# Two float32r parts and paired 64-row matmuls in the attention of a decoder block

## The reference, cut to what matters

```
B, L, D = 4, 1024, 256;  16 heads of 16;  context of 154 tokens;  FFN of 1024
nx = ln(x);  q, k, v = heads(nx @ W_qkv)
x  = x + softmax(q k^T / 4, causal) v @ W_self_out
q  = heads(ln(x) @ W_q);  k, v = heads(context @ W_kv)
x  = x + softmax(q k^T / 4) v @ W_cross_out
x  = x + relu(ln(x) @ W1 + b1) @ W2 + b2
```

## Time and profile before

| | |
|---|---|
| runs | 1325.73 us median of 3 (1321.71 to 1331.97) |
| span of the profiled execution | 1319.6 us (its own time isn't listed beside it) |
| PE busy | 1073.5 us (81%), 7120 matmuls |
| DVE, ACT, POOL busy | 829.3, 644.7, 436.7 us |
| DMA | 115.33 MB, 27% of 16 engines |
| longest entries of the chain | issue 26%, DMA max_rows<-nm 9%, PE L756 8%, PE L737 7% |

### The profile page before, as it was taken

How to read it: one execution, slowest core, us unless ns; L and a number is a source line. 1 busy time by engine, 2 the same in 40 slices (tenths; PEclk the granted TensorE clock), 3 DMA queues, 4 the chain that set the end, 5 groups by cost and what they waited for, 6 DMA issues and landing times.

```text
span 1319.6 us, 23773 instructions
## 1 busy us (share of the span) xinstructions
PE 1073.5 (81%) x7120; PEld 610.3 (46%) x7120; DVE 829.3 (63%) x1489; ACT 644.7 (49%) x1354; POOL 436.7 (33%) x677
## 2 busy tenths in 40 slices
PE   4837768899899989999999574776666889989997
PEld 3625543344344434444337331322222348888886
DVE  6739556688688868888429552543534576666552
ACT  4614335576576756777764242443434572322321
POOL 8624241233233323322334220111111135555443
PEclk9969887899899989999999786877867898999999
DMA  5635333212212221215128431221121311111110
GB/s 160 217 111 147 113 130 105 76 50 86 70 67 78 71 78 62 90 61 178 42 88 264 160 98 51 67 67 60 55 67 60 110 50 48 48 49 62 32 33 32
DMA packets 84521, 115.33 MB, mean 87 GB/s; under 512 B 13632, under 2 KB 70752, under 8 KB 79712
## 3 DMA queue, kind: packets, MB, share of 16 engines
q1 hardware_dynamic: 84416, 114.02, 27.0%
HBM read 71.49 MB, written 42.51 MB: 86 GB/s over the span
## 4 chain that ended last, share of the span: by engine, by line
PE 36%; issue 26%; DMA 17%; POOL 9%; DVE 7%; ACT 3%; SPq 3%; POOLq 0%; DVEq 0%; ACTq 0%
DMA max_rows<-nm 9%; PE bank L756 8%; PE bank L737 7%; PE bank L630 6%; DMA k_st<-k_parts 4%; PE bank L612 3%; PE bank L614 3%; PE bank L613 3%; POOL hT_lo L1516 3%; ACT probs L996 2%; DVE nx_mem L1091 2%; PE bank L633 2%; DMA q_st<-qx_parts 1%; DMA qx_parts<-probs 1%; DVE stats L1080 1%
## 5 line engine op out<-in xcount | busy, mean ns | idle before, releaser
L1105 DVE TENSOR_REDUCE mx<-bank 128x1 f32<-128x512 f32 (+5 forms) x784 | 468.1, 640 | 259.6 <-PE bank L630 133.8
L996 ACT ACTIVATE probs<-bank 128x512 f32<-128x512 f32 (+4 forms) x1024 | 462.6, 518 | 337.6 <-PE bank L737 316.3
L737 PE MATMUL bank<-q_st,k_st 128*128 128x512 bf16 (+4 forms) x1024 | 342.9, 366 | 117.8 <-DMA q_st<-max_rows 100.2
L630 PE MATMUL bank<-k_st,q_st 125*128 125x154 bf16 (+4 forms) x1280 | 311.7, 307 | 74.0 <-DMA k_st<-k_parts 44.7
L737 PEld LDWEIGHTS bank<-q_st,k_st 128*128 128x128 bf16 (+1 forms) x1024 | 102.1, 107 | 338.7 <-ACT probs L996 171.2
L756 PE MATMUL bank<-probs,nx_mem 128*32 128x512 f32 (+4 forms) x2048 | 250.0, 562 | 3.8 <-DVE oT L1181 2.8
L630 PEld LDWEIGHTS bank<-k_st,q_st 125*128 125x128 bf16 x1280 | 129.2, 106 | 149.9 <-DMA k_st<-k_parts 45.6
L1444 POOL TENSOR_SCALAR_AFFINE_SELECT probs<-probs 128x256 f32<-128x256 f32 x256 | 101.2, 407 | 243.1 <-ACT probs L996 240.5
L1516 POOL TENSOR_TENSOR hT_lo<-hT,hT_hi 128x512 fp32r<-128x512 f32 x64 | 93.1, 1474 | 93.4 <-DVE hT_hi L1315 93.4
L1453 POOL TENSOR_TENSOR oN<-oT,rs 128x256 f32<-128x256 f32 x64 | 40.5, 633 | 218.0 <-DVE rs L1186 216.0
L633 PE MATMUL bank<-causal_bf,ident_bf 128*128 128x128 bf16 x512 | 103.7, 227 | 0.0
(11 more groups left out here) (124 smaller groups left out, 1421.0 us busy)
## 6 DMA issues: line engine op xcount, KB each, us to landing
xt<-in_x_dram SPq DMA_DIRECT2D x16, 512.0 KB, 4.9
q_parts<-probs SPq DMA_DIRECT2D x16, 384.0 KB, 3.2
k_parts<-probs SPq DMA_DIRECT2D x16, 384.0 KB, 2.8
q_st<-q_parts SPq DMA_DIRECT2D x16, 384.0 KB
k_st<-k_parts SPq DMA_DIRECT2D x16, 384.0 KB
qx_parts<-probs SPq DMA_DIRECT2D x16, 384.0 KB, 3.4
q_st<-qx_parts SPq DMA_DIRECT2D x16, 384.0 KB
v_aug<-vst_mem SPq DMA_DIRECT2D x8, 544.0 KB, 4.4
```

The costliest lines, as they stand in the source:

```text
L630: last = pe.matmul(bank[:, m, keys * j:keys * j + keys], q_st[w][0:MROWS, i, P * qb:P * qb + P], keys_of(a, w)[0:MROWS, i, k0:k0 + keys], ...
L737: pe.matmul(bank[0:a.kp, m, 0:n], keys_of(a, w)[:, i, a.kp * kb:a.kp * kb + a.kp], q_st[w][:, i, lo:lo + n], start=True, stop=True).then_i ...
L996: act.activation(probs[0:a.kp, use % NPT, 0:n], bank[0:a.kp, a.s_banks[use % a.SB], 0:n], ACT.Exp, scale=SCALE).then_inc(a.exp_done, 1)
L1105: dve.tensor_reduce(mx[:, par, part, blocks.start:blocks[-1] + 1:blocks.step], bank[:, m, 0:len(blocks) * keys].rearrange("p (q k) -> p q ...
```

## The change

q and k are held as two float32r parts; three products of parts (high-high, high-low, low-high) make 48 rows for a head instead of 96. So two heads lie above each other in a stack: head `j` of a pair in partitions 64j to 64j+47, with two rows (48, 49) for two parts of the negated maximum. Weight columns are put in another order for that (`ordered`, `heads`: each ordering is two instructions of half the width). ACT's `middle` and POOL's `lowest` go; DVE's `low` writes the second part itself. A row of a stack is 2 x 1024 x 4 bytes, again 8 KB (2 x 154 x 4 bytes for context keys); a store is 128 rows x 2 parts x 512 tokens x 4 bytes, 512 KB where it was 384 KB. The maxima tiles of a pair of heads go to two banks and one DVE instruction reduces both; S has 20 such units a stack and two units in the ring, X 6 and one unit; the early tiles have one. The masks are made by four bf16 matmuls of 64 rows for a pair. X's accumulator has two banks. DVE negates and splits the maxima in two steps; SP moves them by four DMAs from SBUF to SBUF with no wait between.

```diff
-    NPART = 3
-    Q_PARTS, K_PARTS = (0, 0, 0, 1, 1, 2), (0, 1, 2, 0, 1, 0)
...
+    NPART = 2
+    HALF = P // 2
+    KROWS = 3 * DK
+    KALL = KROWS + NPART
+    RUNS = {"q": ((0, 0, 2, True), (2, 1, 1, False)), "k": ((0, 0, 2, False), (2, 0, 1, False))}
...
-            stacks = [(sb_room(f"q_st{w}", [P, 4, L], BF16), sb_room(f"k_st{w}", [P, 4, L], BF16)) for w in range(4)]
+            stacks = [(sb_room(f"q_st{w}", [P, 2, L], F32R), sb_room(f"k_st{w}", [P, 2, L], F32R)) for w in range(4)]
...
-                            m = min(HF // keys, 4) if keys != 384 else 1
-                            self.tiles += [(range(8 * i + qb, 8 * (i + m), 8), k0, keys, k0 // HF) for i in range(0, 4, m)]
+                            m = min(HF // keys, 2)
+                            self.tiles += [(range(8 * i + qb, 8 * (i + m), 8), k0, keys, k0 // HF) for i in range(0, 2, m)]
...
-        SA = Attention("S", ..., [0, 1, 2], [3], [4, 5, 6, 7])
-        XA = Attention("X", ..., [0, 1, 4, 5], [6], [2, 3, 7])
+        SA = Attention("S", ..., [0, 1, 2], [3], [(4, 5), (6, 7)])
+        XA = Attention("X", ..., [0, 1, 4, 5], [6, 7], [(2, 3)])
-        EARLY_BANKS, EARLY_SLOTS, EARLY_FROM = 3, 12, 20
+        EARLY_UNITS, EARLY_SLOTS, EARLY_FROM = 1, 12, 20
-        EARLY_BANKS_X, EARLY_SLOTS_X, EARLY_FROM_X = 2, 5, 6
+        EARLY_UNITS_X, EARLY_SLOTS_X, EARLY_FROM_X = 1, 5, 6
...
 load_stacks:
-                    for r, first, count in RUNS[side] if side in sides else ():
-                        rows = one(src, u).rearrange("u s (g d i) t -> (u s) g d (i t)", g=2, d=DK)[:, w % 2]
-                        rows = rows[first:first + count] if side == "k" else rows[first:first + 1].to_broadcast([count, DK, 4 * n])
+                    for j in range(2):
+                        for r, first, count, repeated in RUNS[side] if side in sides else ():
+                            rows = one(src, u).rearrange("u s (g j d a) t -> (u s) g j d (a t)", g=2, j=2, d=DK)[:, w % 2, j]
+                            rows = rows[first:first + 1].to_broadcast([count, DK, 2 * n]) if repeated else rows[first:first + count]
+                            p0 = HALF * j + DK * r
...
 rows:
-                sp.wait_ge(a.nm_ready, v + 1)
-                sp.dma_start(max_rows[par].rearrange("s r t -> r s t"), nm[:, par]).then_inc(a.rows_out[par], 16)
-                sp.wait_ge(a.rows_out[par], 16 * (v0 // 2 + 2 * b + 1))
-                sp.dma_start(q_st[v0 % 4][MROWS:P, :, :],
-                             max_rows[par].rearrange("s (i q) t -> s i (q t)", i=4)).then_inc(a.rows_in[par], 16)
+                sp.wait_ge(a.m_free, a.turn_use(v0) + 4 * b * (a.MT + 1) + 1)
+                for j in range(2):
+                    for c in range(NPART):
+                        row = HALF * j + KROWS + c
+                        sp.dma_start(q_st[v0 % 4][row:row + 1, :, :].rearrange("s a (q t) -> s (a q) t", t=P).bitcast(F32),
+                                     nm[16 * j:16 * j + 16, par, c, :].bitcast(F32)).then_inc(a.rows_in[par], 16)
...
 max_tile on PE:
+                for y, (i, qb) in enumerate(divmod(x, 8) for x in blocks):
+                    for j in range(2):
+                        h0 = HALF * j
+                        last = pe.matmul(banks[:, j, keys * y:keys * y + keys], q_st[w][h0:h0 + KROWS, i, P * qb:P * qb + P],
+                                         keys_of(a, w)[h0:h0 + KROWS, i, k0:k0 + keys], start=True, stop=not masked)
                     if masked:
+                        for e0, width in ((HALF, P), (0, HALF)):
+                            for j in range(2):
+                                h0 = HALF * j
+                                last = pe.matmul(banks[:, j, end - width:end], eye[h0:h0 + HALF, e0:e0 + P],
+                                                 below[h0:h0 + HALF, 0:width], start=False, stop=width == HALF)
...
 scores:
-                    pe.matmul(bank[0:a.kp, m, 0:n], keys_of(a, w)[:, i, a.kp * kb:a.kp * kb + a.kp],
-                              q_st[w][:, i, lo:lo + n], start=True, stop=True).then_inc(a.st_ready, 1)
+                    rows = slice(HALF * (i % 2), HALF * (i % 2) + KALL)
+                    pe.matmul(bank[0:a.kp, m, 0:n], keys_of(a, w)[rows, i // 2, a.kp * kb:a.kp * kb + a.kp],
+                              q_st[w][rows, i // 2, lo:lo + n], start=True, stop=True).then_inc(a.st_ready, 1)
...
 slot on PE:
-                    for i in range(4):
-                        if v0 < 4 * B:
-                            scores(v0, b, s, i)
-                        for n in some[(len(some) * i + 3) // 4:(len(some) * (i + 1) + 3) // 4]:
+                    cut = len(some) - len(some) // 2
+                    for pair in range(2):
+                        if v0 < 4 * B:
+                            for i in range(2 * pair, 2 * pair + 2):
+                                scores(v0, b, s, i)
+                        for n in some[cut:] if pair else some[:cut]:
                             max_tile(a, v0 + 2, b, n, a.MB)
-                        if i == 1 and 0 <= q - LAG < 4 * B * a.NS:
+                        if pair == 0 and 0 <= q - LAG < 4 * B * a.NS:
                             weigh((q - LAG) // a.NS, b, (q - LAG) % a.NS)
...
 DVE:
-            def split(ph, use, dst, src, hi):
+            def low(ph, use, part, src):
                 dve.wait_ge(ph.hi_ready, use + 1)
-                dve.tensor_tensor(dst, src, hi, ALU.subtract).then_inc(ph.rest_ready, 1)
+                dve.tensor_tensor(part[:, 1, :], src, part[:, 0, :].bitcast(F32), ALU.subtract).then_inc(ph.lo_ready, 1)
...
-                dve.tensor_scalar(nmf[:, :], bank[0:32, m, 0:P], -1.0, None, ALU.mult).then_inc(a.m_free, 1)
+                dve.tensor_scalar(nm[:, par, 0, :], bank[0:32, m, 0:P], -1.0, None, ALU.mult).then_inc(a.nm_hi, 1)
+                dve.wait_ge(a.nm_hi, v + 1)
+                dve.scalar_tensor_tensor(nm[:, par, 1, :], bank[0:32, m, 0:P], -1.0, nm[:, par, 0, :].bitcast(F32),
+                                         ALU.mult, ALU.subtract).then_inc(a.m_free, 1)
```

More of the change, by code:

```diff
@@ L671, in between @@
                     if early:
[L672 removed]
+                        first_tiles(SA, early[EARLY_SLOTS * hf + j], EARLY_UNITS)
                 for hf in range(2):
@@ L1015, in _ @@
                         high(C, 2 * n + c, parts_c[:, c, 0, :], bank[:, c, :])
-                    for c in range(2):
-                        middle(C, 2, 2 * n + c, parts_c[:, c, 1, :], rest_c[:, c])
             def context_high(b, hf):
@@ L1390, in dense_a @@
                         deviation(A, 2 * (b + 1) + hf, hf)
[L1391 to L1398 removed]
+                    for k in range(KC):
+                        if hf == 0 or more:
+                            tokens_low(2 * b + hf + 1, 1 - hf, k)
             def weights_low(lo, raw, hi, use):
@@ L1487, in dense_c @@
                         deviation(C, n + 2, hf)
-                    for c in range(2):
-                        lowest(C, 2 * n + c, rest_c[:, c], parts_c[:, c, 1, :], parts_c[:, c, 2, :])
-                    if not more and hf == 0:
-                        negated_parts(XA, 0, 0)
             with pool.Fori(0, B - 1) as b:
```

242 lines of the change are left out of this document (96 added, 146 removed).

## The result

The change makes the kernel slower: 1389.9 us, median of 4 runs (1372.5 to 1396.6), against 1326.5 (4 runs, 1321.7 to 1332.0) for the kernel before. The ratio is 1.042, 95% interval 1.034 to 1.049; every ratio in this document leaves out runs more than 1.5% above their kernel's shortest (here the 1396.6), so it isn't quite the quotient of the medians. The prediction was 1233 us, with 1175 to 1300 as its range. The profiled execution of after is the shortest of its four; it has a span of 1370.7 us, 51 more than before, where the medians are 63 apart.

The account below looks back on a forecast made before the run. PE was taken to bound stage S and the DMA queue stage X; gains S 39, X 38, first stacks 9, C 6, last stacks 1 summed to 93 us, so 1319.6 - 93 + 6 = 1233 us, range 1175 to 1300.

Parts of the forecast that it names:

- Paired scores: Stage S, PE: two row halves run at once, 0.22 us a pair; scores 5.3 us a stack instead of 7.7.
- the double bank wait: Stage S, PE: a score pair needs two of three banks free; 0.1 us a step, 1.1 us a stack given back.
- Maxima: Stage S, PE: 24 paired maxima matmuls a stack at 0.22 us, 5.3 us instead of 7.7.
- Masks and weighing: Stage S, PE: masks 2.9 us a stack instead of 1.8, weighing unchanged at 9.5 us.
- Stage S in the sum: Self-attention stage: PE-bound stacks reach 26.1 us, gaining 2.6 us in each of 15, 39 us in all.
- Stage X: Cross-attention stage: queue-bound stacks fall from 19.8 to 16.6 us, 38 us over twelve.
- The last stacks: Stage X: the last three stacks load nothing, so only 1 us is gained.
- first stacks: First stacks of S and X: each loses 2.2 + 2 us of waiting, 9 us together.
- Stage C: Projections in stage C: ACT's cast and POOL's subtraction leave the chain to the store; 6 us shorter, at most 14.
- DVE's reduces: Maxima over two banks: fewer reduces, near 1.2 us for 1024 columns; at most 2.7 us a stack less in S.
- Rival 2: Stage S: pairs run one after the other, 59 us lost there, 1343 us in all; chance 0.08.
- The condition that I named at the end: Stage S: if it gains nothing while pairs overlap, the ring or the double bank wait was underpriced.

Follow-up runs that it names:

- clock_mix: Separate kernel computing nothing of the reference: old and new matmul forms streamed with and without stops; new X step 2.0 us streamed, one every 4.51 us with stops.
- b_64rows: Kernel before with 16-row stack loads, direct row maxima and maxima matmuls over 64 rows instead of 125; 1447.8 us, ratio 1.091.
- a_both: Changed kernel with PE's order of single scores as before and stack loads split into 16-row DMAs over 16 engines; 1280.2 us, ratio 0.969.
- a_single: Changed kernel with PE's order of a step as before, scores no longer in pairs; 1343.6 us in one run (kernel before 1337.1).
- a_spread: Changed kernel with every stack load split into 16-row DMAs, each over 16 engines; 1337.4 us in one run (kernel before 1337.1).
- b_spread: Kernel before with stack loads split into 16-row DMAs over 16 engines, row maxima still through DRAM; 1166.1 us, ratio 0.879.
- b_rows: Kernel before with row maxima sent straight from SBUF to the stack in three DMAs, no DRAM copy or wait; 1282.2 us, ratio 0.966.

## Why the prediction was wrong

**The clock.** No term of the sum and no rival had it: I read the granted clock of 0.98 and 0.76 and carried the durations over as if it came with them. This is the step that failed: the durations were to be those of the full clock, and the granted clock was 0.80 in S and 0.50 in X. Of the 144 us between the span that I forecast and the one measured, S makes 121. Pairs of 48 rows and X's new step lose the clock where PE also stands now and then (clock_mix), and matmuls of half the rows take X from 1.00 to 0.50 (b_64rows). In S the clock costs some 55 us; why it falls there in parts only, and recovers, isn't settled: a_both kept it in S from 446 us on with the same forms, and S's new step kept it in clock_mix, so the forms aren't enough by themselves there. a_single took 41 us off S, a_spread alone added 14, both together took off 77: torn pairs seem to come first and late loads second, but these are single profiles. The cause in S stays open. In X the clock replaces the queue as the bound.

**Paired scores, the double bank wait.** A pair at 0.22 us was right (0.228). The 0.1 us a step for the bank wait was mis-sized. Scores took 10.7 instead of 5.3 + 1.1 us a stack, mostly because PE wants two of three banks while four exponentials a step free them one by one. Some 1.2 us of it is the change from `weigh` to 64-row matmuls, which the prediction put at nothing since the number of changes stays: the number does, the price of 0.10 us is new. Maxima took 1.6 us more than priced; I see lone scores beside them, but haven't split that up. Masks and weighing were right. So S at full clock is at 30.4 us, not 26.1, and even without the order of pairs (28.2 in a_both) it gains 0.5 us where I had 2.6. The kernel before was underpriced as well, 26.7 against 28.7 us, but its sum served only for the difference.

**Stage S in the sum:** −39 us forecast; measured +82, of which +26 by the longer full-clock stack (torn pairs, changes from `weigh` to 64 rows) and some +55 by the clock.

**Stage X:** −38 for twelve stacks forecast, −36 measured for the same twelve (19.9 to 16.9 us each). That is near by luck: I had the queue at 16.0 us, and in the change it is PE at half clock that fills 16.6 of the 16.9 us (a_spread). The last stacks, forecast 1 us shorter, are 8 us longer, since they too are at half clock. I also missed a question: I had found that two or three engines carried a load, and priced only how the change shifts rows between them (34 for the longest instead of 33), not what such a load holds up. b_spread shows that this, not the change's subject, was the 156 us in the span.

**The rest:** first stacks: S's first period 36 us before and 38 after, X's 23.3 and 19.4, so 2 of 9 us came. Stage C was to be 6 us shorter and was 2 longer. Before S, no change was forecast, and it was 1 us shorter. DVE's reduces and the SP order were right.

**The rivals.** Rival 2 came nearest in time (1343 us) but pairs didn't run one after the other; its mechanism is false. The condition that I named at the end, that S gains nothing while pairs overlap, came true, and its reading (the double bank wait underpriced) is at most a third of what S lost.

## What to carry to other kernels

A matmul that uses fewer rows of the array isn't only less work. Read the granted clock beside every term, and make "the clock falls to 1.2 GHz" a rival when the change halves the rows of matmuls in a stage where PE stands now and then; halving work at half clock is no gain. Two matmuls that are to run side by side need both of their output banks at the same moment, so a ring of three fed one at a time tears every second pair. And where a load is seen on two or three of 16 DMA engines, ask first what waits behind it; splitting it to 16-row DMAs was worth 12% here (b_spread), without any new arithmetic. The Trainium skill's rule, that the outermost dimension sets the number of engines (DMA: Bandwidth & Descriptors, "Why a DMA increments its semaphore by 16 and not by 1"), would give such a DMA all 16; the trace agrees with a share of 0.98 during the loads.

## What the runs showed that I had not expected

- A stream of 48-row matmuls in one half of the array, with PE never idle, ran at half clock for the whole 119 us but the first 5; as pairs in both halves it ran at full clock.
- 96 of 128 rows in the maxima changed nothing (0.866 against 0.865); 64 rows took X to half clock.
- A change between 64-row and 128-row matmuls costs 0.10 us each time, and so does one from `weigh` to 64-row matmuls, where one from `weigh` to 128-row matmuls costs nothing.
- Two stops alike didn't do alike: `weigh` with PE busy 58% of the time kept the full clock, pairs of 48 rows with PE busier than that lost it.
- b_rows's X stacks alternate between some 13.7 and 20.3 us (values and stores are issued for two stacks at once; whether that is why wasn't tried). The mean, 16.9, says nothing of it.
